# Gated cross-attention and mixture of experts on one core: queries and keys turned through DRAM and VectorE squares

## What is computed

```python
q = (x @ Wq).reshape(b, n, 32, 16)
k, v = jnp.split(ctx @ Wkv, 2, axis=-1)          # heads of 16
q, k = apply_axial_rope(q, pos), apply_axial_rope(k, pos)
w = jax.nn.softmax(jnp.einsum('bqhd,bkhd->bhqk', q, k) * scale, axis=-1)
attn = jnp.einsum('bhqk,bkhd->bqhd', w, v).reshape(b, n, 512) @ Wout + bout
x = x + jnp.tanh(g_xattn[0]) * attn              # q is made of layernorm(x)
probs = softmax(layernorm(x) @ gate_w.T); weights, selected = top_k(probs, 6)
moe = einsum('te,tei,ehi->th', combine, silu(g) * u, w2)   # g, u = xf @ w1.T
x = x + jnp.tanh(g_ffn[0]) * (moe + shared)
```

## Time and profile before

| | us |
|---|---|
| median of 3 runs | 1397.35 (1395.98 to 1401.92) |
| the profiled execution | 1397.16 |
| its span, from the first to the last instruction | 1395.0 |
| PE busy in the span | 1321.3 (95%) |
| DVE, POOL, ACT busy | 774.5, 697.9, 570.1 |
| granted clock of PE, mean | 0.983 |

### The profile page before, as it was taken

One profiled execution on the slowest core, in us unless ns is written; L12 is line 12 of the kernel. 1 busy time (PEld: TensorE's weight loads), 2 busy tenths in 40 slices (PEclk: granted clock), 3 DMA queues, 4 the chain that ended last, 5 costly groups with the idle time before them and its releaser, 6 DMA issues.

```text
span 1395.0 us, 32586 instructions
## 1 busy us (share of the span) xinstructions
PE 1321.3 (95%) x8414; PEld 1133.8 (81%) x8415; DVE 774.5 (56%) x1572; ACT 570.1 (41%) x1374; POOL 697.9 (50%) x968
## 2 busy tenths in 40 slices
PE   3799999999996898999999999999999999999998
PEld 2566766766764788999999999999999999998887
DVE  4467777777767763444444444444444444356776
ACT  3667667667664422332323333232333323221121
POOL 4354554544545654297442445555542350285673
PEclk9899999999997999999999999999999999999999
DMA  5032332322323665544354444444434443266885
GB/s 202 17 110 83 128 115 80 137 104 80 144 80 108 216 210 182 183 144 133 102 149 146 146 148 144 151 144 141 128 112 148 145 151 85 87 191 206 263 247 157
DMA packets 152398, 196.97 MB, mean 141 GB/s; under 512 B 33155, under 2 KB 103300, under 8 KB 149524
## 3 DMA queue, kind: packets, MB, share of 16 engines
q1 hardware_dynamic: 130292, 104.03, 24.8%
q0 software_dynamic: 22048, 92.23, 19.6%
HBM read 122.11 MB, written 74.07 MB: 141 GB/s over the span
## 4 chain that ended last, share of the span: by engine, by line
PE 75%; DVE 8%; ACT 6%; issue 5%; SPq 2%; DMA 1%; ACTq 0%; DVEq 0%; POOL 0%; POOLq 0%
PE bank L1562 35%; PE bank L1607 19%; PE bank L713 5%; ACT soft L599 4%; PE bank L738 4%; PE bank L1574 3%; PE bank L720 2%; PE bank L752 2%; PE bank L825 2%; DVE smax L1013 2%; PE bank L769 1%; DVE x L1058 1%; DVE attn L1052 1%; DVE stats L1061 1%; SPq L1346 1%
## 5 line engine op out<-in xcount | busy, mean ns | idle before, releaser
L1562 PE MATMUL bank<-w_hi,x_hi 128*128 (+1 forms) x1144 | 289.9, 334 | 0.0
L1562 PE MATMUL bank<-w_hi,x_lo 128*128 (+1 forms) x1144 | 277.1, 323 | 0.0
L1562 PE MATMUL bank<-w_lo,x_hi 128*128 (+1 forms) x1144 | 277.0, 323 | 0.0
L212 POOL CAST w_hi<-w_raw 128x352 fp32r<-128x352 f32 x152 | 72.7, 526 | 369.4 <-PE bank L1562 369.4
L1502 ACT ACTIVATE silu<-bank 128x352 f32<-128x352 f32 x143 | 66.4, 464 | 410.3 <-PE bank L1562 410.3
L1678 DVE SCALAR_TENSOR_TENSOR act<-silu,row_w,bank 128x352 f32<-128x352 f32 x111 | 64.4, 580 | 290.7 <-ACT silu L1502 290.6
L1562 PEld LDWEIGHTS bank<-w_lo,x_hi 128*128 128x128 f32 x1144 | 199.2, 189 | 0.0
L1562 PEld LDWEIGHTS bank<-w_hi,x_lo 128*128 128x128 f32 x1144 | 199.0, 188 | 0.0
L1562 PEld LDWEIGHTS bank<-w_hi,x_hi 128*128 128x128 f32 x1144 | 192.6, 189 | 0.4 <-issue 0.4
L1607 PE MATMUL bank<-w_hi,a_hi 128*128 (+3 forms) x429 | 170.5, 397 | 8.9 <-ACT y L1486 3.8
L599 ACT ACTIVATE soft<-bank,smax 128x128 f32<-128x128 f32 x512 | 146.9, 380 | 76.7 <-DVE smax L1013 76.6
(11 more groups left out here) (186 smaller groups left out, 2155.4 us busy)
## 6 DMA issues: line engine op xcount, KB each, us to landing
xr<-expert_rows SPq DMA_DIRECT2D x444, 64.0 KB, 1.9
y_rows<-y SPq DMA_DIRECT2D x111, 256.0 KB, 2.1
w_raw<-in_w POOLq DMA_DIRECT2D x19, 1408.0 KB, 6.6
w_raw<-in_w POOLq DMA_DIRECT2D x19, 512.0 KB, 7.8
xr<-x_rows SPq DMA_DIRECT2D x88, 64.0 KB, 3.0
x_t<-x_rows SPq DMA_DIRECT2D x22, 256.0 KB, 4.6
x_sb<-in_x SPq DMA_DIRECT2D x16, 256.0 KB, 3.8
x_res<-in_x SPq DMA_DIRECT2D x16, 256.0 KB, 3.0
```

Source lines behind the costliest of these rows:

```text
L212: nc.gpsimd.tensor_copy(w1_hi[d][half][:, s], w1_raw[:, d, halves[half]]).then_inc(w_hi_made, 1)
L1562: last = nc.tensor.matmul(to[:, 0:WIDTH], xx[jt][:, d, :], w[d][half][:, cols], start=(d == 0 and xx is x_hi and w is w1_hi), stop=(d == D ...
```

## The change

From batch 1 on, q and k are no longer turned on PE. SP stores the joined pairs to DRAM (`q_rows`, `k_rows`), waits for that, and loads them back as four quarters each; DVE transposes squares of 32 by 32 into `q_t`, and for k into `k_cos`, from where ACT makes the two copies. For that the heads are laid out in strips of 32 columns, which the host does to the weights' columns. Batch 0 keeps PE's transposes, and POOL writes its pairs in the old order of columns into two other buffers. The v projection moves from u = 7 to u = 5, the copy to `v_one` from u = 7 to u = 6, the two copies to `k_t` from u = 5 to u = 7.

The other parts: small loads are issued by ACT and POOL beside SP, in the order of their use; constants are parted into a first piece and the rest; weights of q and of k, v are split in halves; the angles are made in u = 2 of round 0; the weights out are split in round 1; ACT loads the table of the exponential with a small instruction ahead of round 2; the first matrix of place 1 is split in rounds 4 and 5. In phase B, SP loads before it stores; ACT copies y before the next x_hi in the unrolled steps; DVE adds the early tiles' residual and finishes batches earlier in its step.

```diff
@@ sync
+            def quarters(to, of, landed):
+                for q in range(4):
+                    sp.dma_start(to[32 * q:32 * q + 32, :].rearrange("t (i n) -> t i n", i=4),
+                                 of[:, P * q:P * (q + 1)].rearrange("(i t) n -> t i n", t=32)).then_inc(landed, 16)
+
+            def turn_through_dram(b):
+                waits_apart(sp, passed_sp, (q_rope_done, b + 1))
+                waits_apart(sp, passed_sp, (q_turned, b))
+                sp.dma_start(q_rows, q_rope[:]).then_inc(q_kept, 16)
+                waits_apart(sp, passed_sp, (q_kept, 16 * b))
+                quarters(q_sin, q_rows, q_in)
+                waits_apart(sp, passed_sp, (k_rope_done, b + 1))
+                waits_apart(sp, passed_sp, (k_turned, b - 1))
+                sp.dma_start(k_rows, k_rope[:]).then_inc(k_kept, 16)
+                waits_apart(sp, passed_sp, (k_kept, 16 * b))
+                quarters(k_sin, k_rows, k_in)
...
+                if at(PROJECT) and not first_batch(at(PROJECT)[0]):
+                    turn_through_dram(at(PROJECT)[0])
@@ gpsimd
+            g.dma_start(gate2[:], gates).then_inc(gates_in, 16)
...
                 if isinstance(b, int) and b == 0:
-                    pool.wait_ge(small_in, 16 * 5)
+                    pool.wait_ge(first_in, 16)
...
+                if r == 4:
+                    split_w1(pool, 1, range(0, 2))
+                if r == 5:
+                    split_w1(pool, 1, range(2, 4))
...
                     pool.wait_ge(v_mm, BATCHES)
+                    pool.wait_ge(q_turned, BATCHES)
+                    pool.wait_ge(kt_done, 2 * BATCHES)
                     clear_act()
-                    split_w1(pool, 1)
@@ scalar
+            a.dma_start(const[:, 0:C_FIRST], cf[:, 0:C_FIRST]).then_inc(first_in, 16)
+            a.dma_start(pos_in[:], pos).then_inc(pos_sem, 16)
...
+                    act.wait_ge(tanh_done, 1)
+                    a.activation(gexp[:, 0:2], tanh2[:], ACT.Exp)
...
-                    if at(PROJECT) and u == 3:
-                        b, j, n = at(PROJECT)
-                        act.wait_ge(qt_mm, b + 1)
-                        need(act, score_mm, (b - 1) * GROUPS)
-                        a.activation(q_t[j][:].rearrange("p c n -> p (c n)"), bank[0][:], ACT.Copy)\
-                            .then_inc(qt_done, 1)
...
                     attend(at, u)
-                    if at(PROJECT) and u == 7:
+                    if at(PROJECT) and u == (7 if first_batch(at(PROJECT)[0]) else 6):
                         b, j, n = at(PROJECT)
                         act.wait_ge(v_mm, b + 1)
...
-                    if at(PROJECT) and u == 5:
+                    if at(PROJECT) and u == (5 if first_batch(at(PROJECT)[0]) else 7):
                         b, j, n = at(PROJECT)
-                        act.wait_ge(kt_mm, b + 1)
+                        if first_batch(b):
+                            act.wait_ge(kt_mm, 1)
+                        else:
+                            act.wait_ge(k_turned, b)
                         need(act, score_mm, (b - 1) * GROUPS)
-                        k4 = bank[0][:].rearrange("p (c n) -> p c n", c=DC)
+                        k4 = (bank[0] if first_batch(b) else k_cos)[:].rearrange("p (c n) -> p c n", c=DC)
@@ tensor
                     if u == 0:
-                        pe.wait_ge(qt_done, b + 1)
+                        pe.wait_ge(q_turned, b + 1)
                         pe.wait_ge(kt_done, 2 * (b + 1))
...
-                if u == 3:
-                    pe.wait_ge(q_rope_done, b + 1)
-                    pe.wait_ge(k_rot, 2 * (b + 1))
-                    four_transposes(bank[0], q_rope).then_inc(qt_mm, 1)
+                if u == 3 and first_batch(b):
+                    pe.wait_ge(q_rope_done, 1)
+                    pe.wait_ge(k_rot, 2)
+                    four_transposes(bank[0], first_rope[0]).then_inc(qt_mm, 1)
...
-                if u == 7:
-                    pe.wait_ge(kt_done, 2 * (b + 1))
+                if u == (7 if first_batch(b) else 5):
+                    if first_batch(b):
+                        pe.wait_ge(w_lo_done, 4)
+                        pe.wait_ge(kt_done, 2)
+                    else:
+                        pe.wait_ge(k_rot, 2 * (b + 1))
                     three(bank[0][:], ct, kv_w, CC, lambda t, c: t[:, c, :], lambda w, c: w[:, c, D:2 * D])\
                         .then_inc(v_mm, 1)
@@ vector
+                    if u == 2:
+                        first_angles()
                     if u == 7:
-                        first_angles()
-                        split_weights(0, "q")
+                        split_weights(0, "q0")
...
-                if at(PROJECT) and at(PROJECT)[0] == 1:
-                    if u == 2:
-                        split_weights(2, "o")
+                    if u == 3:
+                        dve.wait_ge(k_rope_done, 1)
+                        split_weights(4, "o")
...
+            def turn_landed(to, landing, landed, b, done):
+                dve.wait_ge(landed, 4 * 16 * b)
+                v.transpose(to.rearrange("p c (i t) -> p i c t", i=4),
+                            landing[:].rearrange("p (i c e) -> p i c e", i=4, c=DC)).then_inc(done, 1)
...
+                    if at(PROJECT) and not first_batch(at(PROJECT)[0]):
+                        if u == 5:
+                            turn_q(*at(PROJECT))
+                        if u == 6:
+                            turn_k(*at(PROJECT))
                     if at(PROJECT) and u == 1:
                         rotate_q(at(PROJECT)[0])
@@ phase_b, sync
+                if i is None or starts_tile(i, 1):
+                    t, j, n = tile(i, at, 1)
+                    if not isinstance(t, int):
+                        load(*at(3))
+                    elif t + 2 < TILES and i != 4:
+                        load(t + 2, j, n + 1)
+                if i == 3:
+                    load(7, 1, 3)
                 if live(i, -2) and (routed(i, -2) or early(i, -2)):
                     store(*at(-2))
...
-                if i is None or starts_tile(i, 1):
-                    t, j, n = tile(i, at, 1)
-                    if not isinstance(t, int):
-                        load(*at(3))
-                    elif t + 2 < TILES:
-                        load(t + 2, j, n + 1)
@@ phase_b, vector
                 if halves_first(i):
                     a_low(*at(-1))
+                    if early(i, -2):
+                        add_early(*at(-2))
...
+                if shared and i in finish_at:
+                    finish(finish_at[i])
                 if shared and i in sum_at:
                     combine_rows(sum_at[i])
```

More of the change, by code:

```diff
@@ L63 @@
 ROUND = 12582912.0
-C_ID, C_UP, C_ONE = 0, 128, 256
-C_IOTA = 384
+C_ID = 0
+C_EVEN = 128
+C_ODD = C_EVEN + 1
+C_P = C_ODD + 1
+C_DUMP = C_P + 1
+C_HALF = C_DUMP + 1
+C_FREQ = C_HALF + 1
+C_FIRST = C_FREQ + 8
+C_UP, C_ONE = C_FIRST, C_FIRST + 128
+C_IOTA = C_ONE + 128
 C_CAP = C_IOTA + 16
@@ L329, in phase_a @@
         x1 = t("x1", [P, D])
+        first_rope = [attn[:].rearrange("p h d -> p (h d)"), x1[:]]
         stats2 = t("stats2", [P, 6])
@@ L349, in phase_a @@
         slots = two("slots", [P, 8], U32)
-        small_in = sem("small_in")
-        w_in = {name: sem(f"w_in_{name}") for name in parts}
+        small_in, first_in, pos_sem, gates_in = sem("small_in"), sem("first_in"), sem("pos_in_sem"), sem("gates_in")
+        w_in = {name: sem(f"w_in_{name}") for name in ("q", "kv", "o")}
+        q_part = [[w.rearrange("p (c n) -> p c n", c=DC)[:, 2 * k:2 * k + 2] for w in parts["q"]] for k in range(2)]
+        kv_part = [[w.rearrange("p (c n) -> p c n", c=CC)[:, :, D * k:D * (k + 1)] for w in parts["kv"]] for k in range(2)]
+        split = {"q0": ("q", q_part[0]), "q1": ("q", q_part[1]), "k": ("kv", kv_part[0]), "v": ("kv", kv_part[1]),
+                 "o": ("o", parts["o"])}
         w_hi_done, w_lo_done = sem("w_hi_done"), sem("w_lo_done")
@@ L362, in phase_a @@
         q_rot, k_rot, q_rope_done, k_rope_done = sem("q_rot"), sem("k_rot"), sem("q_rope_done"), sem("k_rope_done")
-        v_done, qt_mm, qt_done, kt_mm, kt_done = (sem(n) for n in ("v_done", "qt_mm", "qt_done", "kt_mm", "kt_done"))
+        v_done, qt_mm, kt_mm, kt_done = (sem(n) for n in ("v_done", "qt_mm", "kt_mm", "kt_done"))
         score_mm, exp_done, prob_mm, prob_done, pv_mm = (
@@ L396, in phase_a, with first_batch @@
         DEPTH, PEELED = 5, 6
+        def first_batch(b):
+            return isinstance(b, int) and b == 0
         def last_round(at, stage):
@@ L434, in one_round @@
                     sp.wait_ge(v_mm, BATCHES)
+                    sp.wait_ge(q_turned, BATCHES)
+                    sp.wait_ge(kt_done, 2 * BATCHES)
                     sp.wait_ge(x1_out, 16 * EARLY)
@@ L867, in one_round @@
                         score_pair(at, u)
[L868 removed]
+                    if at(PROJECT) and u in (0, 4, 5, 7):
```

(10 more changed lines are left out.)

115 lines of the change are left out of this document (67 added, 48 removed).

## The result

The changed kernel takes 1449.2 us (median of 4 runs, 1447.5 to 1451.4) against 1396.9 us for the kernel before beside it (median of 4, 1396.0 to 1401.9): a ratio of 1.037, 95% interval 1.034 to 1.040. It is slower by 52 us; the forecast was 35 us slower. The profiled execution took 1448.1 us; its span is 51.3 us longer than that of before.

What follows compares the result with a forecast made beforehand. PE was taken to bound most of a round, the score, maximum, exponential loop just behind. Round ends +31, clock +28, other parts -24: +35 us on 1397, so 1432 us, range 1376 to 1457.

Steps and rivals of the forecast that it cites:

- the late k square: Rival: DVE waits for k's transfer and holds the maximum of u = 7; 1.8 us a round, 1457 us, chance 0.10.
- The part u = 4, 5: Steady rounds: k transposes leave PE (0.50 us), the v projection arrives (1.47); from 4.80 to 5.77 us, +0.97 a round.
- The part u = 6, 7: Steady rounds' end: next scores wait for both k copies behind ACT's other work; from 5.41 to 6.67 us, +1.26 a round.
- The clock: PE, short of work at a round's end, loses its full clock: 2.0 us a round, bounds 0 and 3.1, 14 rounds.
- The squares and the trips: DVE's two 0.70 us squares a round and the DRAM trips on SP: taken as 0, trips bounded 0 to 1.8 us.
- q transposes worth 0: Taking q's four transposes from PE in u = 3 buys nothing, as exponentials release the next scores; bounds 0 and 0.5 us.
- The k transposes: Taking k's four transposes from PE in the full part u = 4, 5 saves 0.5 us a round.
- split_w1: Split of place 1 moved from round 17 to the ends of rounds 4 and 5, delaying two turns: +2 us, bounds 0 and +5.
- Start: Before the first scores: small loads spread over queues, angles earlier, weights halved; about 4.3 + 2.2, -6.5 us, bounds -3 and -8.
- Round 17: DVE's 10.26 us x_lo beside POOL's split, with attn and PE behind it, goes: -9.5 us, bounds -8 and -13.
- Early tiles: Loads ahead of stores on SP remove PE's 3.85 us wait at 539.69 and slow running after: -7 us, bounds -3 and -9.
- The rival of the other sign: Rival: ACT's tail at a round's end stays hidden, transposes save 14 x -0.5 = -7 us, no clock loss; 1366 us, chance 0.23.

## Why the prediction was right, and where its sizes were off

*The time:* 1449.2 lies in the stated range, but 1 us above the band given to the forecast itself (1416 to 1448) and in that of the late k square (1445 to 1480). The trace tells the two apart: the rounds pay in the forecast's parts, and no square waits over 0.4 us for its transfer. The sizes below missed mostly to the same side, by 16 us in all.

*The part u = 4, 5:* right, 5.77 forecast, 5.76 measured. The meaning was only half right: I booked it as a loss, and the run with v back shows it as cover for VectorE. Moving v cost nothing.

*The part u = 6, 7:* right in mechanism and order; 6.67 forecast, 6.89 measured. From round 8 to 14 every second round has 7.0; over rounds 7 to 16 the part is 1.54 us longer than before, and not 1.26. The mis-sized term is the k copies. I took 1.26 us from the earlier trace rows, where they read PSUM (0.57 and 0.69); from SBUF they run 272.24 to 273.65, 1.41, and the scores start 0.13 later still, not 0.05. The run with the copies on VectorE brings the part to 5.1.

*The clock:* right, 2.0 forecast, 2.1 measured, in 15 rounds and not in 14, since round 17 starts cold too (1.6 there). The rule of the Trainium skill (TensorE: Matmul & The Clock Gate, section "Why this matters for your kernels"), by which only longer gaps would have mattered, would have kept the clock; the longest gap in a steady round is 2.52 us and the clock fell in each, and in the runs above behind gaps of 0.7. The row at 0.50 was the better guide.

*The squares and the trips:* no delay in the changed kernel, as forecast (k had landed when VectorE came to it at 268.68; a store and the wait for it took about 2.1 us on SP). But the reason given for q ("the scores of u = 6 are ready" only then) was thin: without v in u = 4, 5 the square costs 0.6. The late k, given 0.10, is real where rounds are short.

*q transposes worth 0:* confirmed by the run with q alone. The k transposes: 0.5 fits in the changed kernel, whose part u = 4, 5 is full (5.76); without v in it they were worth 0.2 (4.80 to 4.60), as an exponential ends the part.

*split_w1:* +2 forecast, +5.1 measured (9.59 and 11.06 us where 7.76 stood), at the upper bound. I looked for it in POOL's own queue; it came through VectorE, whose c_lo ran 3.4 and 4.3 us beside the split, as x_lo had in the earlier trace rows. Without turns c_lo comes before the split (in round 5 at 113.30, the split from 114.85), takes 0.42 us, and the two rounds pay 1.6.

*Rounds 3 to 16 in all:* 61.2 forecast, 71.6 measured. Ten steady rounds (7 to 16) at 4.71 and not 4.23 make 4.8 of the missing 10.4, c_lo 3.1, and rounds 3 to 6 the rest, in the main by parts u = 6, 7 that are 1.6 to 1.8 us longer than before and not 1.26.

*Start:* -6.5 forecast, -4.0 measured. The step that failed is xn, which I put 4.3 us earlier. The angles now stand ahead of it on VectorE, and pos lands late; the chain of after and the two waits on PE:

```profile
1.16 6.08 DMA pos_in<-in_pos
```

```profile
10.13 1.08 PE L777 MATMUL bank<-const,xn 128*128 128x128 f32 x4 [10.13 <-DVE xn L1056]
12.82 0.76 PE L770 MATMUL bank<-w_hi,xt_hi 128*128 128x512 f32 x1 [1.60 <-DVE xt_lo L1063]
```

xn came 1.6 us earlier (its transposes at 11.73 before), and xt_lo gave 2.4, where 2.2 were forecast. The run with the angles behind xn has its transposes at 7.64, near the 4.3, but wins only 1.0 at the first scores. With the first turn counted in, -7.9 stands against -8.5.

*Round 17:* the wait behind x_lo, 9.75 us, went but for 0.35 (-9.4, as forecast). The cold start took 1.6 back (6.52, now 8.07) and another fall of the clock at the round's end 1.4 (6.56, now 7.95, at a granted 0.81).

*Early tiles:* the old wait went as forecast: from the first routed tile (523.06, now 583.14) to 548.88 the kernel wins 7.1. Ahead of it a new wait of 5.2 us stands, which I missed:

```profile
554.48 0.32 SPq L499 DMA_DIRECT2D table<-block_table  x1
...
557.75 1.90 SPq L1436 DMA_DIRECT2D xr<-expert_rows  x4
...
563.81 0.43 SPq L1458 DMA_DIRECT2D x_t<-x_rows  x1
```

```profile
566.57 0.69 DVE L1801 TENSOR_TENSOR y<-bank,x_t 128x512 f32<-128x512 f32 x1 [6.66 <-DMA x_t<-x_rows]
```

```profile
569.93 0.90 PE L1668 MATMUL bank<-const,act 128*128 128x128 f32 x3 [5.20 <-DVE act L1772]
```

SP's loads, put ahead of the store, want the table; the store and the load of x1 behind them now wait for it too, VectorE's sum for x1, and the next tile for VectorE. The prediction did not ask what is queued on SP behind a load that waits.

*The rival of the other sign:* the tail, hidden in fact, gives 1392.5 and not 1366; the k transposes were not worth their 7 us, and two squares with their trips cost 13, more than half of it, by the traces, in rounds 4 to 7.

## What to carry to other kernels

Work taken from the engine that bounds a stage buys nothing in the parts where another chain ends it: here, with the v projection at its old step, 8 transposes a round were worth 0.2 us. Work put behind the last instruction of a round, on an engine that runs in order, is paid in full, and where the bounding engine idles for it the clock may be paid as well; ask what a step was hidden by before it is moved. Moving a load ahead of a store moves all that stands behind it past the load's own wait.

## What the hardware showed that was not expected

- The clock at the edge: with the same order of instructions and gaps up to 0.7 us (1.21 and 0.77, or 1.22 and 0.76, us busy in two stretches of 1.70) it stayed in some rounds and fell in others, and with 8 idle transposes for a while in every second one. A fall costs 1.3 to 3.0 us of the next part.
- ScalarE's masked copy of 128x512 took 0.61 us from start to start from SBUF, against 0.57 from PSUM in the earlier trace rows; by its own length 0.80 against 0.69, also within the changed kernel, where batch 0 is copied from PSUM.
- A 128x256 subtraction on VectorE took 0.41 us alone and 3.4 to 5.4 us beside POOL's split of the weights (5.4 in the run with 16 idle transposes). In the changed kernel both ended 0.3 us behind the last of POOL's four subtractions (126.86 behind 126.58, 159.68 behind 159.39): they were held for the whole run of these, not for one.
- A store of 256 KB to DRAM, by the median 2.0 us, took 8.0 once, beside the load of an expert's weights.
